# Layer 0 of a two-layer graph network: position rows loaded from device memory in place of spreading products and copies

## What is computed

```python
# layer 0: each edge adds a weighted row of x (picked by dst) to the node src
gathered = x[dst] * edge_weight[:, None]
pre = segment_sum(gathered, src, num_segments=8192)
x = layernorm(x + pre @ W.T)
# layer 1: a tensor product of x[src] with 9 edge attributes, summed by dst
summand = tensor_product(x[src], edge_attr_9, w0..w4)
x = layernorm(x + segment_sum(summand, dst, 8192) / sqrt(10))
```

## Time and profile before

| | |
|---|---|
| median of 3 runs | 4264.1 us (4263.97 to 4264.62) |
| time of the profiled execution | 4263.51 us |
| its span, first to last instruction | 4261.9 us |
| mean granted TensorE clock | 0.775 |
| busy over the span: PE / DVE / ACT / POOL | 2983.9 / 2178.0 / 1136.9 / 2792.4 us |

### The profile page before, as it was taken

How to read it: one execution, slowest core, us unless ns; L and a number is a source line. 1 busy time by engine, 2 the same in 40 slices (tenths; PEclk the granted TensorE clock), 3 DMA queues, 4 the chain that set the end, 5 groups by cost and what they waited for, 6 DMA issues and landing times.

```text
span 4261.9 us, 66445 instructions
## 1 busy us (share of the span) xinstructions
PE 2983.9 (70%) x19785; PEld 2619.5 (61%) x19786; DVE 2178.0 (51%) x4614; ACT 1136.9 (27%) x2095; POOL 2792.4 (66%) x2939
## 2 busy tenths in 40 slices
PE   2100399999999996776676776676666676676776
PEld 1000299999999995565555655565555555565665
DVE  8999877777777776323323323323323323323443
ACT  5444455555555554100100100100100100100211
POOL 5000177777777773777777777777777777777776
PEclk6555699999999996777777777777777777777777
DMA  1000111111111113222222222222222222222322
GB/s 57 0 0 20 52 51 49 49 49 49 51 49 49 49 49 102 56 56 56 56 56 56 56 56 56 56 56 57 56 56 57 56 56 56 56 56 61 87 81 63
DMA packets 109067, 228.22 MB, mean 54 GB/s; under 512 B 50674, under 2 KB 50818, under 8 KB 107858
## 3 DMA queue, kind: packets, MB, share of 16 engines
q0 software_dynamic: 93744, 194.44, 17.3%
q1 hardware_dynamic: 10658, 24.72, 1.8%
q10 hardware_dynamic: 4608, 8.39, 0.5%
HBM read 212.65 MB, written 8.40 MB: 52 GB/s over the span
## 4 chain that ended last, share of the span: by engine, by line
POOL 37%; issue 13%; PE 7%; DMA 2%; DVE 1%; POOLq 1%; ACT 0%; DVEq 0%; ACTq 0%
POOL feat L1533 37%; PE mixed L1663 3%; PE quad L1648 3%; DMA feat<-x,ids 2%; DVE group L1759 1%; PE attr_t L1614 1%; PE quad L1641 0%; POOLq L1526 0%; POOLq L1530 0%; POOLq L1529 0%; POOLq L1531 0%; ACT ids L1574 0%; DVEq L1759 0%; ACT z_last L1589 0%; PE y L1657 0%
## 5 line engine op out<-in xcount | busy, mean ns | idle before, releaser
L1533 POOL DMA_INDIRECT feat<-x,ids x2048 | 1937.5, 946 | 636.5 <-issue 621.0
L1092 POOL DMA_INDIRECT l_feat<-in_x,id_of x832 | 788.0, 947 | 726.6 <-issue 657.3
L1759 DVE TENSOR_TENSOR group<-group,quad 128x504 f32 (+1 forms) x512 | 348.1, 680 | 1723.6 <-PE quad L1648 1689.1
L1648 PE MATMUL quad<-attr_hot,feat 128*128 128x144 f32 x4096 | 809.6, 354 | 490.4 <-DMA feat<-x,ids 490.4
L1648 PEld LDWEIGHTS quad<-attr_hot,feat 128*128 128x128 f32 x4096 | 679.9, 235 | 631.1 <-DMA feat<-x,ids 380.1
L1663 PE MATMUL mixed<-group,mix 128*128 128x192 f32 x2304 | 678.5, 479 | 235.0 <-DVE group L1759 235.0
L1663 PEld LDWEIGHTS mixed<-group,mix 128*128 128x128 f32 x2304 | 637.6, 301 | 278.0 <-issue 247.0
L1574 ACT CAST ids<-src_col 128x8 int32 (+1 forms) x256 | 50.6, 197 | 2178.3 <-PE quad L1648 2178.3
L1738 DVE TENSOR_TENSOR attr_hot<-hot,attr_t 128x1152 f32<-128x1152 f32 x256 | 346.5, 1354 | 9.0
L1179 PE MATMUL got<-x_near,far_w 128*128 128x128 bf16 x5376 | 350.2, 220 | 1.2 <-DVE far_w L988 0.8
L997 DVE TENSOR_SCALAR w_row<-swap,src_of,w_of 128x184 f32<-128x184 f32 x1024 | 327.3, 389 | 0.1
(11 more groups left out here) (258 smaller groups left out, 3198.5 us busy)
## 6 DMA issues: line engine op xcount, KB each, us to landing
feat<-x,ids POOLq DMA_INDIRECT x2048, 2.5
l_feat<-in_x,id_of POOLq DMA_INDIRECT x832
attr_in<-in_edge_attr SPq DMA_DIRECT2D x129, 72.0 KB
norm_x<-in_x SPq DMA_DIRECT2D x16, 256.0 KB, 2.7
x<-norm_z ACTq DMA_DIRECT2D x16, 256.0 KB, 2.4
x_t<-x SPq DMA_DIRECT2D x15, 256.0 KB, 3.2
out<-z_t ACTq DMA_DIRECT2D x15, 256.0 KB, 2.4
keys<-far_keys SPq DMA_DIRECT2D x2, 512.0 KB, 3.2
```

The lines of the kernel that those rows point to most:

```text
L1092: pool.indirect_dma_start(feat[:, landing, :], None, x, bass.IndirectOffsetOnAxis(ap=id_of[s % 2][:, c:c + 1], axis=0)).then_inc(feat_in[l ...
L1533: pool.indirect_dma_start(feat[z][:, t, :], None, x1, bass.IndirectOffsetOnAxis(ap=ids[z][h][:, t % H:t % H + 1], axis=0),).then_inc(feat_ ...
L1648: last = nc.tensor.matmul(bank[:, :, bass.ds(places[t % H], WIN)], feat[z][:, t, :], attr_hot[h][:, t % H, :, :], start=False, stop=(t % Q ...
L1759: nc.vector.tensor_tensor(to, to, quad[:, q, 0:NA * QUAD_WIN].rearrange("p (m n) -> p m n", m=NA), ALU.add).then_inc(quad_added, 1)
```

## The change

The spreading products and the copies go. The position rows of all fetched tiles are stored to device memory once, ahead of the loop, ordered so that the 19 rows of one part lie side by side. In the loop SP loads the 19 rows of a part into all 128 partitions by one transfer (`to_broadcast`), into one of two buffers `place[0]`, `place[1]` (s even, s odd). `near` and `rest` read them there and wait for the load once a part (`wait_places`). `pos` is made earlier on VectorE. PSUM, free of `place_b`, takes a second `got`, so a fetch no longer waits for the message just before it. `g.ident_bf` goes too.

On SP, after the wait for the starts and ahead of their store:

```diff
             sp.wait_ge(starts_made, 1)
-            spot = stage.rearrange("a b -> (a b)")[0:R * OFFS]
+            table = stage.rearrange("a b -> (a b)")
+            spot = table[0:R * OFFS]
+            words = P // 2
+            spread = table[SPREAD_AT:SPREAD_AT + R * L * len(PLACED) * words]
+            by_quad = spread.rearrange("(t s m e) -> m s t e", t=R, s=L, e=words)
+            sp.wait_ge(pos_made, 1)
+            for m, c in enumerate(sorted(PLACED)):
+                own = pos[c * L:(c + 1) * L, :].bitcast(F32).rearrange("s (t e) -> s t e", e=words)
+                sp.dma_start(by_quad[m], own).then_inc(spread_out, 16)
             sp.dma_start(spot.rearrange("(t v) -> t v", t=R), starts_i[:].bitcast(F32)).then_inc(starts_out, 16)
             sp.wait_ge(starts_out, 16)
             sp.dma_start(starts_row[0:1, :].bitcast(F32), spot.unsqueeze(0)).then_inc(starts_in, 16)
+            sp.wait_ge(counts_made, 1)
+            n_turns, n_src = loop_counts(sp)
+            sp.wait_ge(spread_out, 16 * len(PLACED))
+            by_part = spread.rearrange("(a f) -> a f", a=R * L)
...
+                        with sp.Fori(0, R) as t:
+                            for s in range(LH):
+                                k = group_no(wd, ws, hf, t, s, 0)
+                                sp.wait_ge(near_made, k + (NEAR0 - GROUPS))
+                                sp.wait_ge(rest_made, k + (NEAR0 - GROUPS))
+                                sp.dma_start(place[s][:].bitcast(F32),
+                                             by_part[bass.ds(t * L + (hf * LH + s), 1)].to_broadcast([P, len(PLACED) * words])
+                                             ).then_inc(placed[s], 16)
```

The buffers, the wait and ScalarE's step:

```diff
+        place = [sb(f"place{z}", [P, len(PLACED) * P], BF16) for z in range(LH)]
-        place_b = ctx.enter_context(nc.psum_tensor("place_b", [P, 2 * BANK], F32))
-        got = ctx.enter_context(nc.psum_tensor("got", [P, 2 * BANK], F32))
+        got = [ctx.enter_context(nc.psum_tensor(f"got{z}", [P, 2 * BANK], F32)) for z in range(2)]
...
+        def wait_places(eng, wd, ws, hf, t, s, j):
+            if j == 0:
+                eng.wait_ge(placed[s % LH], (wd * PS + ws) * (HALVES * R * 16) + (hf * R + t) * 16 + 16)
...
-            def rest(k, j):
+            def rest(k, s, j):
-                act.wait_ge(placed, k + 1)
-                act.wait_ge(near_made, k + 1)
-                used = NF[j] * P
-                nc.scalar.copy(place[z][:, 0:used], place_b[:, 0:used]).then_inc(copied, 1)
-                act.wait_ge(copied, k + 2)
-                act.wait_ge(rest_made, k + 2)
-                nc.scalar.activation(rest_far[:, cols], place[z][:, cols], ACT.Abs, bias=not_wanted[which - 2]
+                act.wait_ge(rest_made, k + NEAR0)
+                nc.scalar.activation(rest_far[:, cols], placed_at(s, j, cols), ACT.Abs, bias=not_wanted[which - 2]
```

On VectorE and TensorE:

```diff
             dve.wait_ge(cols_cast, 2)
+            nc.vector.tensor_scalar(pos[:], dst_f, g.span_from[:, 1:2], None, ALU.subtract).then_inc(pos_made, 1)
             dve.wait_ge(miss_shown, 1)
...
-            nc.vector.tensor_scalar(pos[:], dst_f, g.span_from[:, 1:2], None, ALU.subtract).then_inc(pos_made, 1)
...
-                dve.wait_ge(copied, k + 2)
...
-            def spread(k, t, lane_s, j):
-                pe.wait_ge(copied, k + 1)
-                for m, i in enumerate(FETCHED[j]):
-                    v = (j * GROUP + i) * L + lane_s
-                    lane = g.ident_bf[:, v:v + 1].to_broadcast([P, P])
-                    last = nc.tensor.matmul(place_b[:, m * P:(m + 1) * P], lane, pos[:, bass.ds(t * P, P)], start=True,
-                                            stop=True)
-                last.then_inc(placed, 1)
...
-                        last = nc.tensor.matmul(got[:, cols], hot, rows, start=(n_done == 0),
+                        last = nc.tensor.matmul(got[z][:, cols], hot, rows, start=(n_done == 0),
...
-                pe.wait_ge(msg_made, k + 2)
+                pe.wait_ge(msg_made, k + 3)
...
-                                if later:
-                                    spread(k + 2, later[1], later[0] * LH + later[2], later[3])
```

More of the change, by code:

```diff
@@ L585, in first_edges @@
         feat_in = [sem(f"l_feat_in{i}") for i in range(RING)]
-        placed = sem("placed")
-        copied = sem("copied")
+        spread_out = sem("spread_out")
+        placed = [sem(f"placed{z}") for z in range(LH)]
         near_made = sem("near_made")
@@ L612, in holding, with placed_at @@
             return [m for m, i in enumerate(FETCHED[j]) if c in BLOCKS[PLACED[j * GROUP + i]]]
+        def wait_places(eng, wd, ws, hf, t, s, j):
+            if j == 0:
+                eng.wait_ge(placed[s % LH], (wd * PS + ws) * (HALVES * R * 16) + (hf * R + t) * 16 + 16)
+        def placed_at(s, j, cols):
+            first = sum(NF[0:j]) * P
+            return place[s % LH][:, first + cols.start:first + cols.stop]
         def columns(picked):
@@ L714, in _ @@
             sp.dma_start(starts_row[0:1, :].bitcast(F32), spot.unsqueeze(0)).then_inc(starts_in, 16)
+            sp.wait_ge(counts_made, 1)
+            n_turns, n_src = loop_counts(sp)
+            sp.wait_ge(spread_out, 16 * len(PLACED))
+            by_part = spread.rearrange("(a f) -> a f", a=R * L)
+            with sp.Fori(0, n_turns) as wd:
+                with sp.Fori(0, n_src) as ws:
+                    for hf in range(HALVES):
+                        with sp.Fori(0, R) as t:
[6 more added lines that the diff above has]
+                                             ).then_inc(placed[s], 16)
         @block.scalar
@@ L827, in slots @@
                                 h = part_no(wd, ws, hf, t, s)
-                                if next_group(hf, t, s, j, 2, last):
-                                    rest(k + 2, (j + 2) % GROUPS)
+                                ahead = next_group(hf, t, s, j, 2, last)
+                                if ahead:
+                                    wait_places(act, wd, ws, *ahead)
+                                    rest(k + 2, *ahead[2:])
                                 later = next_group(hf, t, s, j, GROUPS, last)
@@ L1027, in slots @@
                                 h = part_no(wd, ws, hf, t, s)
-                                if next_group(hf, t, s, j, 2, last):
-                                    near(k + 2, (j + 2) % GROUPS)
+                                ahead = next_group(hf, t, s, j, 2, last)
+                                if ahead:
+                                    wait_places(dve, wd, ws, *ahead)
+                                    near(k + 2, *ahead[2:])
                                 later = next_group(hf, t, s, j, 1, last)
@@ L1132, in _ @@
                     pe.wait_ge(cols_made, 1)
[L1133 removed]
+                    nc.tensor.transpose(got[1][0:R, 0:P], first[:], ident).then_inc(first_turned, 1)
                 if b == 8:
@@ L1145, in _ @@
                     pe.wait_ge(miss_made, 1)
-                    nc.tensor.matmul(place_b[:, 0:2], ones[:], miss[:], start=True, stop=True).then_inc(miss_shown, 1)
-            pe.sem_inc(near_made, 2)
+                    nc.tensor.matmul(got[0][:, 0:2], ones[:], miss[:], start=True, stop=True).then_inc(miss_shown, 1)
+            pe.sem_inc(near_made, NEAR0)
             pe.sem_inc(got_made, 2)
@@ L1223, in slots @@
                                 k = group_no(wd, ws, hf, t, s, j)
-                                later = next_group(hf, t, s, j, 2, last)
-                                if later:
-                                    spread(k + 2, later[1], later[0] * LH + later[2], later[3])
                                 if next_group(hf, t, s, j, 1, last):
```

49 lines of the change are left out of this document (23 added, 26 removed).

## The result

| | before | after |
|---|---|---|
| median of 4 runs each | 4264.03 us (4262.53 to 4264.62) | 4226.86 us (4225.72 to 4227.90) |
| ratio, with its 95% interval | | 0.9913 (0.9896 to 0.9930) |
| time of the profiled execution, its span | 4263.51, 4261.9 us | 4227.08, 4225.3 us |
| loop's first sums start | 514.31 us | 519.88 us |
| loop's last sums start | 1622.1 us | 1585.6 us |

The change is faster by 4264.03 - 4226.86 = 37.2 us, or 0.87%. The forecast was 63 (4264 - 4201). All of it lies in the loop: the last sums start 1622.1 - 1585.6 = 36.5 us earlier. From first to last sums the loop took 1107.8 us and now takes 1065.7, so it lost 42.1 us where 67.0 were forecast; 5.6 us went at its start, where 4.1 were.

What follows compares the result with a forecast made beforehand. TensorE was taken to bound layer 0's group loop at 17.45 us a part, GpSimd second at 16.24. 4263.5 - 67.0 (spreading products) + 4.1 (later beginning) = 4200.6, against the median 4201; range 4190 to 4240.

Steps and rivals of the forecast that it cites:

- the likeliest case: The main forecast for the whole kernel: 4201 us, own range 4190 to 4212, chance 0.68.
- The spreading products: TensorE in layer 0's group loop: removing 1,216 products, 19 a part, saves 1.055 us a part, 67.0 us after the beginning.
- Double buffering of the fetched rows: TensorE's fetches no longer wait for the message before; those waits were 0.4 us in all, so nothing in the loop.
- the time isn't freed: Rival: TensorE's gap before sums grows by up to 0.26 us if spreading products hid register loads; 4264 us, chance 0.05.
- A gap over 0.2 us in every group: The sign, between TensorE's fetch and sums, that was to show the rival of time not freed.
- The gap itself: TensorE's 0.13 us between a fetch's last step and the first sum, taken as its own issuing.
- The beginning: Loop's start: 19 stores issued ahead of the starts delay first sums from 514.31 to near 518.4 us, 4.1 us late.
- The stores hold the beginning: Rival: stores at the loop's start drain at 38 us instead of 10.5, delaying the starts; 4228 us, chance 0.10.
- The loads bound the loop: Rival: position loads above 17.45 us each make VectorE and ScalarE wait; up to 5130 us, chance 0.05.
- the estimate of 0.12 more: DMA engines in the loop: 64 loads, 39.8 MB, add 0.12 to a busy share of 0.18, leaving gathers room.
- GpSimd becomes the bound: Rival: gathers slowed beside the loads make a part take 16.9 us in the loop; 4233 us, chance 0.12.
- the margin of 1.2 us a part: GpSimd's 16.24 us a part against TensorE's 17.45 before the change; TensorE savings beyond that can't be had.

Runs made afterwards that it cites:

- One buffer: The changed kernel with the doubling of the fetched rows undone, one `got` buffer and the old message counts: 4206.85 us, ratio 0.9862 to the kernel before.
- the first experiment: The changed kernel with two semaphores' counts shifted, so fetch and sums wait on the same register value: 4198.43 us, ratio 0.9847; run again 4197.26 us.
- places first in the changed kernel: The changed kernel with the load of the places moved ahead of the fetch: 4203.94 us, ratio 0.9854 to the kernel before.
- one more in either kernel: One-hot rows' count started at 20, so the sums' wait needs its own register value: kernel before 4284.21 us, changed kernel 4246.45 us (one run).

## Why the prediction was right and wrong

**Direction and range: right, the range in part by luck.** The time fell inside 4190 to 4240, but outside the likeliest case's own range of 4190 to 4212. The upper end was set for the rivals of GpSimd and of the stores, and neither came; the 25 us that filled the room came from a term priced at nothing.

**The spreading products: right.** They were worth what was forecast. The fetch follows the sums directly (the last sums of a group start at 1008.02 and the fetch at 1008.33, two steps of sums later), and where the register instruction is away the kernel takes 4198, against the 4201 forecast.

**The failed step is "Double buffering of the fetched rows", priced at "nothing in the loop".** It looked at what the wait releases and not at what the wait is made of. Its value moved from k + 2 to k + 3; that is an addition more behind each fetch, 0.097 us in each of 256 groups, 25 us. The waits that the price rested on the earlier trace rows can't show it. The code could: two waits that compared with one value before don't share it after. "One buffer" gives the term its right size: not 0, but some 22 us of cost by the ratios, 25 by the gap.

**The rival "the time isn't freed": its sign, not its cause.** "A gap over 0.2 us in every group" came (in 247 of 255), and the rival's price was a bound for it: 0.26 us a group, where 0.10 came. But its reason, that the spreading products hide the register loads, fell: with them in place an instruction more cost 20 us, and without them the gap went back to 0.13.

**The gap itself** was taken as fixed ("TensorE's own issuing"). It was the load of the places, 0.59 us on TensorE's queue, whose row of before stands in no term of the sum. Moving it ahead of the fetch removes all of the gap, in either kernel.

**The beginning: right in kind, 1.5 us short in this execution.** All engines around it (start, us, engine, line), which answers to the earlier trace rows:

```profile
493.80 1.29 DVE L985 TENSOR_SCALAR pos<-swap,span_from 128x2048 bf16<-128x2048 f32 x1 [0.16 <-DVE edge_miss L981]
...
496.42 8.16 SPq L728 DMA_DIRECT2D table<-pos  x19
504.63 0.34 SPq L729 DMA_DIRECT2D table<-starts_i  x1
506.49 0.25 SPq L731 DMA_DIRECT2D starts_row<-table  x1
508.57 0.21 DVE L1042 TENSOR_SCALAR turn_f<-turn_f 128x1 f32<-128x1 f32 x1 [9.36 <-DMA starts_row<-table]
509.07 13.11 SPq L745 DMA_DIRECT2D place<-table  x3
...
514.05 0.40 DVE L1016 TENSOR_SCALAR far_w<-place,cst 128x512 bf16<-128x512 bf16 x1 [4.33 <-DMA place<-table]
...
515.37 2.08 PE L1201 MATMUL got<-x_near,far_w 128*128 128x128 bf16 x18 [10.68 <-DVE far_w L1017]
```

The stores were issued in 8.16 us, 0.43 each, under the 0.55 taken and between the bounds of 0.32 and 0.59. The first load came out at 509.07, 1 us earlier than forecast, but took until some 514.0 to land: 4.9 us, where 3.6 were forecast (the two rows of 2.7 us for 256 KB and 3.2 for 512 continue to 3.4, not 3.6). The first fetch begins at 515.37 (forecast 514.8), the sums at 519.88 (518.4). But executions with this same beginning differ by more than that: in the first experiment the first load was issued at 508.76 and waited for until 514.1, 5.3 us; when the same kernel ran again, at 508.36 and until 512.1, 3.7 us, and its first sums started at 518.24. So one execution doesn't show that a load of one row into all partitions is slower than the rows it was continued from.

**"The stores hold the beginning": fell.** The store of the starts, queued behind the 19, was waited for only until their load could be issued, 506.49 - 504.63 = 1.9 us after it. The rule of the Trainium skill behind that rival ("DMA: Bandwidth & Descriptors", section "Why a DMA increments its semaphore by 16 and not by 1": the slowest dimension sets the number of engines, four here) may hold all the same: no run shows which engines carried the stores. What didn't follow is the 38 us, which a full gather packet's time, 126 ns, for each 256 B run gave. From 497.20 to 506.00 us, when the runs moved, the 16 engines were busy for a share of 0.24: 0.24 x 16 x 8.80 / 1216 = 28 ns a run at most, under the 35 ns that the prediction named as deciding. Even on four engines that is 304 x 28 ns = 8.5 us, about what the issuing took.

**"The loads bound the loop": fell,** as the run without them shows. Who waited for them, over the whole loop (us, times), and their issues:

```profile
L745 SPq DMA_DIRECT2D place<-table x64: 332/337/383, 509.1 to 1541.3; - x64
...
  ACT far_keys L831: 7.5, 1
  DVE far_w L1016: 4.3, 1
```

One wait each, at the beginning. The DMA engines' share of the loop rose from 0.18 to 0.29, as the estimate of 0.12 more said, and a gather stayed at 950 ns on the mean (947 before, 950 without the loads).

**"GpSimd becomes the bound": not in the change,** where TensorE waited for no gather. The 59 waits for sums in the row above (18.0 us) are the usual gaps of 0.3 us, but the 57 late starts, 51 of them behind GpSimd's wait for the sums ahead of a group's first gather, lie 26 us in all beyond that gap (134 with 64 us before): it still had slack. But the margin of 1.2 us a part was read rightly: where TensorE gains more than the 67 us (places first in the changed kernel), it waits for gathers.

## What to carry to other kernels

When a change alters the number in a wait, ask what else used that number. Before taking work off the fullest engine, find the pace of the second: here 1.249 us a gather put a floor under every version with 13 gathers a part, as far as the profile shows.

## What the runs showed of the hardware

A load of eight values from SBUF into registers holds TensorE's queue for 0.59 us. An addition of registers takes 0.032 us there, but behind such a load it put the sums off by 0.09 to 0.10 us: 25 us for 256 of them (the change), 28.4 for 288 (the first experiment), 20.2 and 19.6 for 224 (one more in either kernel). With the load ahead of the fetch it cost nothing. Its 0.032 us is not its price: the next instruction of the queue starts 0.092 us after the addition does (median of 256 in the change; 0.093 of 253 in the kernel before with one more), which is about what the sums came later. The Trainium skill ("Advanced Engine Details and Errata", section "Sequencer and Instruction Queues") says that the sequencer reads the next instruction and pushes those for the engine into a queue, where they wait until they can run. The trace agrees, with the load's start 0.86 us ahead of the end of the products before it; but a load of 0.59 us and what follows it use more than that lead. Why the next instruction starts only 0.06 us after the addition has ended, no run shows.

A load of one 4,864 B row into 128 partitions took 3.7 to 5.3 us from issue to the end of the wait for it at the loop's beginning, and 64 of them (39.8 MB) moved beside the gathers without slowing them (950 ns a gather with and without). A store of 64 runs of 256 B from four partitions took SP 0.39 us to issue in the median, and 19 in a row held up the store behind them by no more than their issuing.
